# Second attention of a four-stage kernel: values of the heads turned in 32x32 squares by VectorE, TensorE's order changed

## The reference

```
Q = [x W_DQ W_UQ, rope(x W_DQ W_QR)]   K = [x W_DKV W_UK, rope(x W_KR)]   V = x W_DKV W_UV
scores  = clip(Q K^T, -80, 80), causal mask
weights = softmax(scores / sqrt(12))
out     = (weights V, heads side by side) @ W_O
```

## Time and profile before

| | us |
|---|---|
| median of 3 runs (lowest, highest) | 2088.64 (2086.4, 2090.76) |
| profiled execution, its own time | 2088.71 |
| span from its first to its last instruction | 2087.0 |

### The profile page before, as it was taken

How to read it: one execution, slowest core, us unless ns; L and a number is a source line. 1 busy time by engine, 2 the same in 40 slices (tenths; PEclk the granted TensorE clock), 3 DMA queues, 4 the chain that set the end, 5 groups by cost and what they waited for, 6 DMA issues and landing times. The chain is left out here.

```text
span 2087.0 us, 40191 instructions
## 1 busy us (share of the span) xinstructions
PE 2011.9 (96%) x14693; PEld 1351.3 (65%) x14693; DVE 1642.2 (79%) x3987; ACT 1436.7 (69%) x1936; POOL 616.3 (30%) x865
## 2 busy tenths in 40 slices
PE   5999999999999999997899999999999997999998
PEld 3777777777777777776444444777777773444443
DVE  5998888988889888874676675777777766999997
ACT  3877888777887778874677776566666664555554
POOL 2444544444444444542000000333333330000000
PEclk9999999999999999998999999999999998999999
DMA  2400000000000000002655453000000000000000
GB/s 87 113 14 21 21 22 20 13 22 21 21 22 11 22 21 21 22 11 63 127 123 118 104 107 82 1 2 2 2 2 2 2 2 1 11 16 11 16 16 16
DMA packets 55362, 69.38 MB, mean 33 GB/s; under 512 B 13008, under 2 KB 32640, under 8 KB 55168
## 3 DMA queue, kind: packets, MB, share of 16 engines
q1 hardware_dynamic: 55168, 66.82, 13.8%
HBM read 45.30 MB, written 4.72 MB: 24 GB/s over the span
## 5 line engine op out<-in xcount | busy, mean ns | idle before, releaser
L908 POOL TENSOR_SCALAR_AFFINE_SELECT pr<-pr 128x512 f32<-128x512 f32 x256 | 202.3, 813 | 370.5 <-ACT pr L831 370.5
L453 PE MATMUL a_pO<-va,pr 128*128 128x66 f32 x2048 | 303.3, 271 | 1.9 <-POOL pr L908 1.5
L453 PEld LDWEIGHTS a_pO<-va,pr 128*128 128x128 f32 x2048 | 272.5, 192 | 18.9 <-issue 15.4
L1735 ACT ACTIVATE c_pr<-c_pS 128x1536 f32<-128x1536 f32 x128 | 185.9, 1452 | 119.4 <-PE c_pS L1542 119.4
L1790 POOL TENSOR_SCALAR_AFFINE_SELECT c_pr<-c_pr 128x512 f32<-128x512 f32 x256 | 158.0, 641 | 261.6 <-DVE c_pr L1655 261.6
L797 ACT ACTIVATE sq<-a_pW 128x512 f32<-128x512 f32 x192 | 114.4, 597 | 147.8 <-PE a_pW L394 145.2
L825 ACT ACTIVATE th<-a_pS 128x1536 f32<-128x1536 f32 x128 | 185.9, 1452 | 30.1 <-PE a_pS L438 29.6
L454 PE MATMUL a_pO<-va,pr 128*128 128x66 f32 x1024 | 198.2, 275 | 0.0
L831 ACT ACTIVATE pr<-th 128x1536 f32<-128x1536 f32 x128 | 190.4, 1488 | 3.1
L438 PE MATMUL a_pS<-qs,k 128*128 128x512 f16 (+1 forms) x1024 | 187.3, 326 | 0.9 <-issue 0.9
L1655 DVE TENSOR_SCALAR c_pr<-c_pr 128x1536 f32<-128x1536 f32 x128 | 122.6, 958 | 76.9 <-ACT c_pr L1735 76.9
(11 more groups left out here) (246 smaller groups left out, 4415.2 us busy)
## 6 DMA issues: line engine op xcount, KB each, us to landing
b_cwB<-b_by_expert SPq DMA_DIRECT2D x64, 512.0 KB, 8.4
k<-k SPq DMA_DIRECT2D x64, 256.0 KB, 3.7
x<-in_L_attn_tokens_dram SPq DMA_DIRECT2D x8, 512.0 KB, 7.2
out_dram<-x SPq DMA_DIRECT2D x16, 256.0 KB, 2.3
d_h<-in_L_ffn_h_w_dram SPq DMA_DIRECT2D x2, 1024.0 KB, 7.1
b_by_expert<-b_cwT SPq DMA_DIRECT2D x64, 8.0 KB, 1.8
wmod<-in_L_wmod_dram SPq DMA_DIRECT2D x2, 384.0 KB, 3.6
d_w<-in_L_ffn_w_w_dram SPq DMA_DIRECT2D x3, 256.0 KB, 3.3
```

What stands on the lines that cost most here:

```text
L453: pe.matmul(out, w[:, hh * N + t * P:hh * N + (t + 1) * P], v[:, 0, p, :], start=True, stop=t == 0)
L908: last = gp.affine_select(out=part, in_=part, compare_op=ALU.is_ge, fill=0.0, base=0, pattern=[[0, HPG], [1, P]], channel_multiplier=-1)
L1735: act.activation(pr[g][:, :, :], pS[:, :, 0:N + P], ACT.Exp, scale=float(1.0 / np.sqrt(np.float32(DQ)))).then_inc(s_ex, 1)
```

## The change

The eight transposes of `pe_heads_back` and the two of `pe_heads_turned` go, with ACT's copy `act_take_heads` and both `dve_normalise`. In their place DVE turns `vu` in squares of 32x32, in place within each band of 32 partitions: two instructions of 512 columns (`dve_turn_values`), one reciprocal of 32 columns, one multiplication of 256 (`dve_divide`), one transpose of 256 columns into `at` (`dve_turn_back`). Because squares stay in their band, the heads are dealt to the bands in another order: head hh*4+g instead of g*4+hh, which changes `attention1_take` (from 7 ACT instructions to 25, of smaller pieces) and the slice of `va` that PE loads.

PE's order: the first projection now stands ahead of the output projection, the second projection moves from behind the weighted values to behind the third scores, beside the third projection; `pe_out_back` gets the wait for the addition that `pe_heads_back` had. DVE's order changes to match. In `measure` the third step goes: `bn_aggr` writes `mv` itself, in all three stages that use it, and the counts in waits on `s_st` follow.

```diff
-ADD_STEPS = 4
+ADD_STEPS = 3
...
-    elif step == 2:
+    else:
         dve.wait_ge(s_st, ADD_STEPS * n + 2)
         for t in range(tiles):
-            last = dve.bn_aggr(c.agg[:, t, :], c.stat[:, t, :])
-    else:
-        dve.wait_ge(s_st, ADD_STEPS * n + 3)
-        last = dve.tensor_copy(c.mv[:, n * tiles:(n + 1) * tiles, :], c.agg[:, 0:tiles, :])
+            last = dve.bn_aggr(c.mv[:, n * tiles + t, :], c.stat[:, t, :])
...
 def attention1_take(act, products, bank):
...
-    act.activation(wq[:, :, 0:DC], bank[:, 0:HD].rearrange("p (h d) -> p h d", d=DC), ACT.Copy)
-    act.activation(wk[:, :, 0:DC], bank[:, HD:2 * HD].rearrange("p (h d) -> p h d", d=DC), ACT.Copy)
     act.activation(wv[:, :], bank[:, 2 * HD:3 * HD], ACT.Copy)
-    for b in range(4):
-        act.activation(wq[:, :, DC + b:DC + 4 * DR:4],
-                       bank[:, 3 * HD:3 * HD + H1 * DR].rearrange("p (h d) -> p h d", d=DR), ACT.Copy)
+    for s in range(HPG):
+        heads = [bank[:, at + s * HD // HPG:at + (s + 1) * HD // HPG].rearrange("p (g d) -> p g d", d=DC) for at in (0, HD)]
+        act.activation(wq[:, s, :, 0:DC], heads[0], ACT.Copy)
+        act.activation(wk[:, s, :, 0:DC], heads[1], ACT.Copy)
+        turned = bank[:, 3 * HD + s * H1 * DR // HPG:3 * HD + (s + 1) * H1 * DR // HPG].rearrange("p (g d) -> p g d", d=DR)
+        for b in range(4):
+            act.activation(wq[:, s, :, DC + b:DC + 4 * DR:4], turned, ACT.Copy)
...
         def pe_out_back(pe, n):
             pe.wait_ge(s_og, n + 1)
+            if n >= 1:
+                pe.wait_ge(s_st, ADD_STEPS * (n - 1) + 1)
...
                 if 0 <= n < B:
                     pe_scores(pe, n, 0)
+                if 0 <= n + 1 < B:
+                    pe_project(pe, n + 1, 0)
                 if 0 <= n - 2 < B:
                     pe_out_project(pe, n - 2)
                 if 0 <= n + 1 < B:
-                    pe_project(pe, n + 1, 0)
                     pe_values(pe, n + 1)
                 if 0 <= n < B:
                     pe_scores(pe, n, 1)
                 if 0 <= n - 1 < B:
                     pe_weighted_values(pe, n - 1, 1)
-                if 0 <= n + 1 < B:
-                    pe_project(pe, n + 1, 1)
+                if 0 <= n - 2 < B:
+                    pe_out_back(pe, n - 2)
                 if n == -1:
                     pe_turn_following(pe, 4)
-                if 0 <= n - 2 < B:
-                    pe_out_back(pe, n - 2)
                 if 0 <= n < B:
                     pe_scores(pe, n, 2)
-                if 0 <= n - 1 < B:
-                    pe_heads_back(pe, n - 1, 0)
-                if 0 <= n + 1 < B:
+                if 0 <= n + 1 < B:
+                    pe_project(pe, n + 1, 1)
                     pe_project(pe, n + 1, 2)
                 if n == -1:
                     pe_turn_following(pe, 5)
-                if 0 <= n - 1 < B:
-                    pe_heads_back(pe, n - 1, 1)
                 if 0 <= n < B:
                     pe_scores(pe, n, 3)
                     pe_weighted_values(pe, n, 0)
-                if 0 <= n - 1 < B:
-                    pe_heads_turned(pe, n - 1)
...
+        def dve_turn_values(dve, n, half):
+            dve.wait_ge(s_vu, 2 * n + half + 1)
+            if n >= 1:
+                dve.wait_ge(s_nm, n)
+            these = slice(2 * half, 2 * half + 2)
+            dve.transpose(vT[:, these, :, :].rearrange('p g j w -> p (g j w)'), vu[n % 2][:, these, :].rearrange('p g i -> p (g i)')).then_inc(s_vT, 1)
+
+        def dve_reciprocals(dve, n):
+            dve.wait_ge(s_vT, 2 * n + 2)
+            if n >= 1:
+                dve.wait_ge(s_nm, n)
+            dve.reciprocal(rl[:, :, :], vT[:, :, :, DC]).then_inc(s_rl, 1)
+
+        def dve_divide(dve, n):
+            dve.wait_ge(s_rl, n + 1)
+            if n >= 1:
+                dve.wait_ge(s_at, n)
+            dve.tensor_tensor(an[:, :, :, :].rearrange('p j g d -> p g j d'), vT[:, :, :, 0:DC],
+                              rl[:, :, :].unsqueeze(3).broadcast_to((P, groups, N // SQ, DC)), ALU.mult).then_inc(s_nm, 1)
+
+        def dve_turn_back(dve, n):
+            dve.wait_ge(s_nm, n + 1)
+            if n >= 1:
+                dve.wait_ge(s_o, n)
+            dve.transpose(at[:, :], an[:, :, :, :].rearrange('p j g d -> p (j g d)')).then_inc(s_at, 1)
```

More of the change, by code:

```diff
@@ L1492, in attention1 @@
         vu = [sb(f'vu{k}', [P, groups, N]) for k in range(2)]
-        rl = sb('rl', [P, TT, H1])
-        an, at, og = sb('an', [P, TT, H1, DC]), sb('at', [HD, N]), sb('og', [D, N])
+        SQ = 32
+        vT = sb('vT', [P, groups, N // SQ, VW])
+        rl = sb('rl', [P, groups, N // SQ])
+        an, at, og = sb('an', [P, N // SQ, groups, DC]), sb('at', [HD, N]), sb('og', [D, N])
         pS = ctx.enter_context(nc.psum_tensor('c_pS', [P, HPG, BANK], F32))
@@ L1499, in attention1 @@
         s_sc, s_ex, s_cl, s_mk, s_pv, s_vu = (sem(x) for x in ('sc', 'ex', 'cl', 'mk', 'pv', 'vu'))
-        s_aT, s_rl, s_nm, s_bT, s_at, s_o, s_og, s_oT, s_st = (
-            sem(x) for x in ('aT', 'rl', 'nm', 'bT', 'at', 'o', 'og', 'oT', 'st'))
+        s_vT, s_rl, s_nm, s_at, s_o, s_og, s_oT, s_st = (
+            sem(x) for x in ('vT', 'rl', 'nm', 'at', 'o', 'og', 'oT', 'st'))
         block = ctx.enter_context(nc.Block())
@@ L1555, in pe_weighted_values @@
                     for hh in range(HPG):
-                        last = pe.matmul(pC[hh * VW:(hh + 1) * VW, j * N + keys * P:(j + 1) * N], va[n % 3][:, keys, g * HPG + hh, :],
+                        last = pe.matmul(pC[hh * VW:(hh + 1) * VW, j * N + keys * P:(j + 1) * N], va[n % 3][:, keys, hh * groups + g, :],
                                          pr[g][:, hh, keys * N:keys * N + N - keys * P], start=keys == 0, stop=keys == TT - 1,
@@ L1559, in pe_weighted_values @@
             last.then_inc(s_pv, 1)
[L1561 to L1576, removed]
         def pe_out_project(pe, n):
@@ L1686, in _ @@
                     dve_take_heads(dve, n, 3)
+                if 0 <= n - 1 < B:
+                    dve_turn_values(dve, n - 1, 0)
                 if 0 <= n + 2 < B:
@@ L1695, in _ @@
                     dve_take_heads(dve, n + 1, 0)
+                if n == -1:
+                    dve_take_following(dve, 4)
                 if 0 <= n < B:
@@ L1699, in _ @@
                     dve_add(dve, n - 2)
+                if 0 <= n - 1 < B:
+                    dve_turn_values(dve, n - 1, 1)
                 if 0 <= n + 1 < B:
                     dve_take_heads(dve, n + 1, 1)
-                if n == -1:
-                    dve_take_following(dve, 4)
                 if 0 <= n - 2 < B:
@@ L1714, in _ @@
                     dve_take_following(dve, 5)
+                if 0 <= n - 1 < B:
+                    dve_divide(dve, n - 1)
+                if 0 <= n - 2 < B:
+                    dve_measure(dve, n - 2, 2)
+                if 0 <= n < B:
+                    dve_clip(dve, n, 2)
+                if 0 <= n - 1 < B:
+                    dve_turn_back(dve, n - 1)
                 if n == 2:
@@ L1738, in act_take_values @@
             act.wait_ge(s_pv, 2 * n + half + 1)
-            if half == 0 and n >= 2:
-                act.wait_ge(s_aT, 2 * n - 2)
+            if n >= 2:
+                act.wait_ge(s_vT, 2 * n - 3 + half)
             act.activation(vu[n % 2][:, 2 * half:2 * half + 2, :].rearrange('p g i -> p (g i)'), pC[:, :], ACT.Copy).then_inc(s_vu, 1)
-        def act_take_heads(act, n):
-            act.wait_ge(s_bT, n + 1)
-            if n >= 1:
-                act.wait_ge(s_o, n)
-            act.activation(at[:, :], pD[:, 0:N], ACT.Copy).then_inc(s_at, 1)
         def act_place_values(act, n):
```

40 lines of the change are left out of this document (11 added, 29 removed).

## The result

| | before | after |
|---|---|---|
| median, us (runs) | 2089.25 (4) | 2058.53 (4) |
| lowest to highest | 2086.4 to 2090.76 | 2056.16 to 2060.06 |
| profiled execution, its own time | 2088.71 | 2060.06 |
| span | 2087.0 | 2058.3 |

The ratio is 0.9851, 95% interval 0.9838 to 0.9864: 30.7 us less by the medians, where 33.5 were forecast (2055; range 2048 to 2067). In a later comparison (five runs of it, eleven of before) the same kernel stood at 2057.65 beside 2091.25, ratio 0.984 (0.9815 to 0.9865), 33.6 us less.

A forecast was written before the change was run, and what follows sets the result against it. PE, busy throughout the second attention, was taken as the bound; 31.6 + 0.9 + 0.75 + 1.2 + 0.55 - 1.5 = 33.5 us off 2088.7 gives 2055 us, range 2048 to 2067.

The forecast's parts named there:

- PE's sum: PE, one second-attention batch: 12.93 less 1.33 for ten transposes plus 0.24 for new neighbours, 11.84 us.
- DVE's sum: DVE, one second-attention batch: 9.47 us becomes 10.5 of PE's 11.84, so DVE stays below PE.
- The line through rows of other operations: DVE's square transposes: 0.311 for 128 columns plus 0.13 per further 128, giving 0.70 and 0.44 us.
- the proportional one (1.24): DVE's square transposes, dear end: four and two times the 128-column 0.311, 1.24 and 0.62 us.
- the first rival: DVE mildly becomes the bound through dear transposes: 12.1 us a batch for 11.84, 2063 us; chance 0.12.
- Scores and exponentials: PE's score groups, at least 2.59 us apart: new distances 2.81, 2.66, 2.79, 3.58 all exceed it, cost nothing.
- The margin of 0.07: Second to third scores on PE: distance 2.66 us, above the least distance 2.59 by 0.07 only.
- the second rival: Second-to-third scores lose their 0.07 because of ACT: 0.15 to 0.3 us a batch, 2060 to 2064; chance 0.05.
- Waits that could take over: Each engine's batch laid out: PE waits for none; heads of group 3 release the values' bank 0.9 us early.
- The rival on the other side: DVE holds PE up at the values' bank from 1.7 us per 512-column transpose; 2111 us at 2.0; chance 0.04.
- VectorE beside POOL: Clip 3 may meet a POOL mask, allowed 0.37 us; the exposed division runs between masks and adds nothing.
- Outside the steady part: 29 batches gain 31.6 us; start 0.9, last iterations 0.75, tail 1.2, `mv` copies 0.55 gained; take 1.5 lost.

The follow-up runs named there:

- the doubled kernel: Changed kernel with each of the two 512-column square transposes a batch on DVE issued twice: 2058.99 us, ratio to before 0.9846.
- PE's old order: Changed kernel with the second projection back behind the weighted values and the output projection ahead of the first: 2079.04 us, ratio to before 0.9947.
- the tripled kernel: Changed kernel with each of the two 512-column square transposes a batch on DVE issued three times: 2067.2 us, ratio to before 0.9888.
- the repetition: The changed kernel as it is, run and traced a second time: 2057.65 us, ratio to before 0.984.
- the take in 7: Changed kernel with ACT's `attention1_take` in 7 instructions again for 25, heads dealt out by PE's column reads: 2057.91 us, ratio to before 0.9845.
- The removed copies alone: Kernel before with only the third step of `measure` removed, `bn_aggr` writing `mv` itself: 2090.79 us beside 2091.66, ratio 0.9994.

## Why the prediction was right, by its own steps

- **PE's sum.** Forecast 11.84 a batch, measured 11.84. Counting starts instead of durations, and charging each block by its new neighbours (+0.24), carried it. Without the neighbours the batch would have come out at 11.60 and the time some 7 us too low. The borders came as priced: 0.97 for the fourth and the second projection, 0.95 for the third, 0.36 for the turn back. (The prediction calls the projection at 1455.75 the third; it is the fourth, and the sum uses it as that.)
- **DVE's sum.** The square transposes were put at 0.70 and 0.44 and took 0.704 and 0.439; the reciprocal 0.336 for 0.36, the division 0.412 for 0.42. The busy sum was 10.5 and is 10.2. The line through rows of other operations was the right reading, the proportional one (1.24) wrong. With it, the first rival would have been near; the doubled kernel puts about as much on DVE (2 x 0.61) and its steady batches stay at 11.84, so even then no wait would have come.
- **Scores and exponentials.** The distances are 2.80, 2.67 and 2.79 (forecast 2.81, 2.66, 2.79), and PE waits for none of the exponentials. The margin of 0.07 sufficed, and the second rival did not come about. PE's old order shows what a distance below 2.59 costs.
- **Waits that could take over.** The values' bank was named as the place and as having 0.9 us to spare; in the steady batches of the changed kernel the heads of group 3 end 1.3 us early (1452.17 for 1453.45), and the tripled kernel's steady batches wait there for DVE and nowhere else. The rival on the other side put DVE's decisive point at 1.7 us a transpose by DVE's busy time; by the tripled kernel DVE's need is some 0.6 us lower than that, so its point lies still further out. What the forecast put at nothing was DVE's work that comes once: in the iteration with `ln_scales` PE does wait at this bank, and that batch gives back 0.7 us of the gain. The 29 batches brought 375.16 - 344.52 = 30.6 us, not 31.6.
- **VectorE beside POOL.** Clip 3 was allowed 0.37 and takes 1.24 where the others take 0.96, 0.28 more, and POOL's masks of clips 2 and 3, which it meets, take 3.12 in a row where two pairs alone take 2 x 1.23 (the changed kernel's timelines):

```profile
1450.34 1.25 DVE L1635 TENSOR_SCALAR c_pr<-c_pr 128x1536 f32<-128x1536 f32 x1
```

```profile
1450.13 3.12 POOL L1783 TENSOR_SCALAR_AFFINE_SELECT c_pr<-c_pr 128x512 f32<-128x512 f32 x4 [3.25 <-DVE c_pr L1635]
1454.70 1.23 POOL L1783 TENSOR_SCALAR_AFFINE_SELECT c_pr<-c_pr 128x512 f32<-128x512 f32 x2 [1.45 <-DVE c_pr L1635]
```

  PE's wait for them stays at nothing. The Trainium skill ("SBUF — State Buffer", "Who interferes with whom") says that where a VectorE instruction in a two-port mode and a GpSimd one want the pair of ports that they share, the one issued first has it for its whole length and the other is blocked. The trace agrees, in the order of the starts: a mask runs from 1450.13 at its usual 0.64; clip 3, begun 0.2 behind it, takes 0.28 longer than the others; the second mask, begun during the clip, takes 1.36 for 0.64; and the first instruction of the front, begun during the last mask, 0.60 for the 0.30 that it has behind the masks. The division, exposed by the skill's rule that the prediction cites, runs at 0.408 to 0.425 in all 32 cases and never meets a mask, as it was placed; so no run here shows what it would cost. The squares do meet masks, 63 of the 64 of 512 columns, and take no longer for it (0.695 to 0.715, the one alone 0.705).
- **Outside the steady part.** The stage was to give 31.6 + 0.9 + 0.75 + 1.2 + 0.28 = 34.7 us. The profiled execution has 33.1, with 1.6 lost to the lower clock, which the forecast did not foresee; the repetition has 34.6. That the repetition agrees so well is partly luck: 1.0 too much in the 29 batches stands against 0.5 too little before the third scores of batch 1 (27.09 to 25.70 us) and 0.3 in the tail (4.46 to 3.00). The take was mis-sized. 1.5 was forecast (its own bullet works out 1.3); the trace has 0.7 with the removed copy in it, and 0.95 against the take in 7. Pieces of 16 and 32 columns follow each other by 0.06 and 0.08 (20 steps from 1307.50 to 1308.89) and not by 0.09. Up to the first scores nothing of it is left, 11.46 us for 11.53.
- **The remaining 3.5 us** between 2055 and 2058.5 are no more than the stages outside scatter by, which the change hardly touches: +3.7 in this pair of traces (1.6 of it in the first attention), +2.8 with the repetition, all of it in the first attention. (The forecast's own range comes out of its bounds at 2048 to 2062, not 2049 to 2061; nothing hangs on it.) The last steps of the first attention ran with a granted clock of 0.66 in 970 to 980, for 0.83 in the trace of before. The removed copies alone, which have the same first attention, also start their experts later than the profiled run of before. That the change causes it is not shown: the kernel with PE's old order has the same first attention and starts its experts 3.4 us earlier than before, and the later comparison has 33.6 us less, so scatter is the likelier reason. That 33.6 meets the forecast of 33.5 so closely is luck too, as its interval is some 10 us wide.

## What to carry to other kernels

Where one engine is busy throughout a stage, price what is taken from it by the distance of starts and by its new neighbours, and then lay the new order of every engine out over one period: here the order alone brought nothing and taking the transposes away alone a third, and only both together the whole. A resource used once per group (one tile of scores and its exponential) sets a least distance, and work must be dealt out so that each gap is just above it. Look over more than one period as well: work that comes once (here `ln_scales`) can use up a slack that every other batch has. Where instructions of an engine grow beside another engine's, its busy time overstates its need: doubling and tripling its work tells the slack.

## Not expected of the hardware

- DVE's 32x32 square transposes of f32 columns: 311 ns for 128, 439 for 256, 704 for 512, about 1.02 ns a column above a fixed 0.18 us, from start to start 0.61 for 512.
- These squares take no longer beside POOL's masks, while clips of 1536 columns take 1.24 us for 0.96 there and the mask that meets them 1.36 for 0.64.
- ACT's small copies out of PSUM follow each other by 0.06 us (16 columns), 0.08 (32), 0.10 (64) and 0.16 to 0.17 (128), so the take in 25 pieces cost only 1 us more than in 7 at the boundary (2.5 for 1.54), and 0.3 of it by the first scores.
- PE's granted clock fell to its lower level (1.2 of 2.4 GHz) in four of six traces behind a wait of 1.65 us near the start of the stage: third to fourth scores took 4.42 us instead of 2.79. Behind a wait of 1.66 near the stage's end it fell in two of eight. Both gaps came with the change: the second projection, which had filled the first, was moved, and the transposes that had stood in the second went.
